# Phase B of a decoder layer on one core: another order of the slots around the step boundary

## The reference, cut to what matters

```
xn  = rmsnorm(layernorm(x)) ; mn = rmsnorm(memory)
q   = rope(xn @ q_w[h])            4 heads of 128
k   = rope(mn @ kv_w[0]) ; v = mn @ kv_w[1]      one head, shared
p   = softmax(mask(q @ k.T))       per head 512 x 512
enc = p @ v ;  out = x + sum_h enc[h] @ out_w[h]
```

## Time and profile before

| | |
|---|---|
| median of 3 runs | 3421.82 us (3419.85 to 3423.12) |
| profiled execution | 3417.78 us, its span 3416.0 us |
| mean granted PE clock | 0.976 |
| busy share of the span | PE 95%, PEld 79%, DVE 53%, ACT 40%, POOL 30% |
| phase B | about 1015 to 2045 us of the span, steps of 63.92 us |

### The profile page before, as it was taken

How to read it: one execution, slowest core, us unless ns; L and a number is a source line. 1 busy time by engine, 2 the same in 40 slices (tenths; PEclk the granted TensorE clock), 3 DMA queues, 4 the chain that set the end, 5 groups by cost and what they waited for, 6 DMA issues and landing times. The chain is left out here.

```text
span 3416.0 us, 41523 instructions
## 1 busy us (share of the span) xinstructions
PE 3231.5 (95%) x15856; PEld 2696.0 (79%) x15856; DVE 1814.0 (53%) x3793; ACT 1357.4 (40%) x2576; POOL 1024.2 (30%) x838
## 2 busy tenths in 40 slices
PE   7999999999958999999999987999999999999799
PEld 5888888888747878878878866888888888888687
DVE  5666666565547777777777754322322232221464
ACT  4444444444336666666666642221112111111233
POOL 1323232323226566565565540000000000000134
PEclk9999999999979999999999996999999999999899
DMA  2111112121131211211211103000000000000343
GB/s 102 38 52 60 59 53 69 43 73 39 50 107 52 88 64 51 88 64 51 88 64 51 62 25 112 24 24 14 13 13 25 13 13 13 25 1 0 127 161 135
DMA packets 102341, 188.28 MB, mean 55 GB/s; under 512 B 6912, under 2 KB 13056, under 8 KB 102144
## 3 DMA queue, kind: packets, MB, share of 16 engines
q1 hardware_dynamic: 102144, 185.63, 16.1%
HBM read 135.28 MB, written 50.33 MB: 54 GB/s over the span
## 5 line engine op out<-in xcount | busy, mean ns | idle before, releaser
L949 POOL TENSOR_SCALAR b_soft<-b_soft,b_one_in_sum 128x512 f32<-128x512 f32 x256 | 401.0, 1566 | 336.5 <-DVE b_one_in_sum L1116 336.5
L1490 ACT ACTIVATE c_gate<-c_g,c_bias 128x512 f32<-128x512 f32 x180 | 124.2, 690 | 754.1 <-PE c_g L131 754.1
L1513 DVE TENSOR_TENSOR c_gate<-c_gate 128x512 f32<-128x512 f32 x64 | 44.3, 692 | 570.9 <-ACT c_gate L1490 570.9
L287 POOL TENSOR_TENSOR kept_scale<-c_ln_ve,minus_half 128x4 f32<-128x4 f32 x16 | 16.1, 1009 | 961.9 <-DVE c_ln_ve L279 961.9
L1135 DVE TENSOR_TENSOR b_p_lo<-b_t,b_p_hi 128x512 fp32r<-128x512 f32 x256 | 175.1, 684 | 198.9 <-ACT b_p_hi L1001 197.1
L992 ACT ACTIVATE b_soft<-b_soft,b_minus_top 128x512 f32<-128x512 f32 x256 | 185.2, 724 | 232.0 <-DVE b_minus_top L1127 227.3
L480 ACT ACTIVATE a_elu<-a_p 128x512 f32<-128x512 f32 x128 | 76.5, 598 | 345.3 <-PE a_p L131 298.5
L1001 ACT ACTIVATE b_p_hi<-b_t 128x512 fp32r<-128x512 f32 x256 | 152.5, 596 | 102.4 <-PE b_t L1285 102.3
L1285 PE MATMUL b_t<-ident,b_soft 128*128 128x128 f32 x1024 | 157.8, 277 | 23.7 <-DVE b_p_lo L1135 23.7
L1660 POOL TENSOR_TENSOR d_x<-d_x,d_y 128x512 f32<-128x512 f32 x64 | 83.0, 1296 | 321.4 <-ACT d_y L1673 321.4
L1127 DVE CUSTOM_DVE_ANT_0 b_soft<-b_l,b_mask_row 128x512 f32<-128x512 f32 x256 | 175.2, 685 | 0.0
(11 more groups left out here) (303 smaller groups left out, 10153.5 us busy)
## 6 DMA issues: line engine op xcount, KB each, us to landing
a_x<-in_x SPq DMA_DIRECT2D x16, 1024.0 KB, 8.2
a_res<-in_x SPq DMA_DIRECT2D x16, 1024.0 KB, 6.4
x<-a_res SPq DMA_DIRECT2D x16, 1024.0 KB, 5.2
b_mem<-in_ctx SPq DMA_DIRECT2D x16, 1024.0 KB, 5.4
b_x<-x SPq DMA_DIRECT2D x16, 1024.0 KB, 5.5
b_res<-x SPq DMA_DIRECT2D x16, 1024.0 KB, 5.5
x<-b_res SPq DMA_DIRECT2D x16, 1024.0 KB, 4.3
c_x<-x SPq DMA_DIRECT2D x16, 1024.0 KB, 5.5
```

Source lines behind the costliest of these rows:

```text
L949: pool.tensor_scalar(soft[:, at, :], soft[:, at, :], one_in_sum[:, at:at + 1], None, ALU.mult).then_inc(p_norm.sem, p_norm.unit)
L1490: act.activation(gate[:, j % 2, i, :], gating.banks[(3 * j + i) % 6][:, :], ACT.Tanh if g == "c" else ACT.Sigmoid, bias=added[:, i, j:j + ...
```

## The change

Three moves, made alike on PE, ACT and DVE. `encode(old, 2)` goes from slot 15 to slot 14, and its `enc_high`/`enc_low` from slot 0 of the next step to slot 15. `encode(fin, 3)` goes from slot 1 to slot 0, `keys_values(0)` and `(1)` from slots 0 and 2 to slots 1 and 2, with the copies that follow them. The second pair of memory transposes goes from slot 14 to slot 15, and its `memory_high`/`memory_low` from slot 15 to slot 0 of the next step. `norm_apply` of tiles 2 and 3 moves from slot 2 to slot 1. No instruction is added or taken away.

```diff
@@ ACT
                         if fin:
                             if j == 0:
                                 p_high(fin.b, J - 1)
-                                enc_high(fin.b, 2)
-                            if j == 2:
+                            if j == 1:
                                 enc_high(fin.b, 3)
                         if old:
...
+                            if j == 15:
+                                enc_high(old.b, 2)
                         if new:
-                            if j == 1:
-                                values_high(0)
-                            if j == 3:
-                                values_high(1)
+                            if j == 0 and new.b >= 1:
+                                memory_high(s - 1, new.b, 2)
+                                memory_high(s - 1, new.b, 3)
+                            if j == 2 or j == 3:
+                                values_high(j - 2)
...
-                            if j == 14 or j == 15:
-                                memory_high(s, after, 2 * (j - 14))
-                                memory_high(s, after, 2 * (j - 14) + 1)
+                            if j == 14:
+                                memory_high(s, after, 0)
+                                memory_high(s, after, 1)
@@ PE
-                        if new and j == 0:
-                            keys_values(0)
-                        if fin and j == 1:
+                        if fin and j == 0:
                             encode(fin, 3)
-                        if new and j == 2:
-                            keys_values(1)
+                        if new and j in (1, 2):
+                            keys_values(j - 1)
...
-                        if following(new, B) and j in (13, 14):
-                            turn_memory(s, new.b + 1, 2 * (j - 13))
-                            turn_memory(s, new.b + 1, 2 * (j - 13) + 1)
-                        if old and j == 15:
+                        if following(new, B) and j in (13, 15):
+                            turn_memory(s, new.b + 1, j - 13)
+                            turn_memory(s, new.b + 1, j - 12)
+                        if old and j == 14:
                             encode(old, 2)
```

More of the change, by code:

```diff
@@ L1203, in step @@
                         if fin:
-                            if j == 0:
-                                enc_low(fin.b, 2)
-                            if j == 2:
+                            if j == 1:
                                 enc_low(fin.b, 3)
@@ L1212, in step @@
                                 enc_low(old.b, 1)
+                            if j == 15:
+                                enc_low(old.b, 2)
                         if new:
[L1214 to L1217, removed]
+                            if j == 0 and new.b >= 1:
+                                memory_low(s - 1, new.b, 2)
+                                memory_low(s - 1, new.b, 3)
+                            if j == 2 or j == 3:
+                                keys(j - 2)
                             if 4 <= j <= 7:
@@ L1243, in step @@
                                 self.norm_variance(dve, N, after)
-                            if j == 14 or j == 15:
-                                memory_low(s, after, 2 * (j - 14))
-                                memory_low(s, after, 2 * (j - 14) + 1)
+                            if j == 14:
+                                memory_low(s, after, 0)
+                                memory_low(s, after, 1)
                             if j == 15:
```

## The result

| | before | after |
|---|---|---|
| median | 3420.84 us (3419.81 to 3423.12, 4 runs) | 3441.61 us (3438.33 to 3446.04, 4 runs) |
| ratio | | 1.0061, 95% interval 1.0043 to 1.0078 |
| profiled execution, span | 3417.78, 3416.0 us | 3440.21, 3438.5 us |
| mean granted PE clock | 0.976 | 0.970 |

Slower by 0.6%, by the mechanism that was forecast and inside the range, with the price of the clock too small and the term for the ends of the wrong sign. The waits of PE in the steady part, as in the earlier trace rows: of the three old kinds none is left but b_t on p_lo, which has grown, and b_e on p_lo is new.

The account below looks back on a forecast made before the run. PE, busy 95% of the span, was taken to bound the kernel, losing 2.95 us per boundary to waits. Order +3.5, ends -1.6 and clock +9.6 gave +11.5 on 3417.78 us, 3433 us on the median; range 3418 to 3445.

Parts of the forecast that it names:

- the price of the clock: PE at a boundary where the clock falls to its lower level: 1.6 us per fall, range 0.9 to 1.9.
- the term for the ends: First and last boundaries of phase B, outside the steady ones: together -1.6 us.
- Slot 14 and slot 15: PE: encode(old, 2) hides slot 14's waits, but turn_p(15) stays at 1470.90 behind p_low(14), a stall of 1.71 us.
- Slots 0 to 2: PE: encode(fin, 3) stalls 1.48 us for p_low(15), until 1473.57; turn_x at 1485.48 against 1485.23, +0.25 us per boundary.
- the boundary into the step without a new item: End of phase B: gets the wait for p_low(15) with no keys to fill it, +0.7 us (0 to +1.5).
- the last step: End of phase B: shorter wait for enc_low(2) before encode(fin, 3), -1.3 us (0 to -2.0).
- the first boundary: Start of phase B, no fin: waits within keys_values(0) partly covered by the new order, -1 us (between 0 and -2.8).
- The clock: Steady boundaries: waits of 1.71 and 1.48 us close together make PE's clock fall at 6 of 14, +9.6 us.
- The sum: Whole kernel: +3.5 - 1.6 + 9.6 = +11.5 us on the profiled execution of 3417.78 us; chance 0.50.
- The clock that holds: Rival, steady boundaries: every boundary keeps the clock, +1.9 us, 3423.7 us, no measurable change; chance 0.30.
- The hidden waits: Rival, slots 15 and 0: p_low(14) and p_low(15) come as soon as transposes allow, -30 us, 3392 us; chance 0.08.
- The collision of DVE and POOL: Rival: POOL's L949 holds up norm_apply of the first tile, delaying p_low(15) by 0.45 us; +6.3, 3439 us; chance 0.12.

Follow-up runs that it names:

- the swap alone: Kernel before with only encode(old, 2) and the second memory turns exchanged between slots 14 and 15, head 2's copies in slot 15: 3417.89 us, ratio 0.9995.
- both waits filled: Changed kernel plus unused matmuls, 4 ahead of turn_p(15) and 5 ahead of encode(fin, 3): 3424.89 us, ratio 1.0015.
- the late copies: Changed kernel with the first two memory copies (high and low) moved from slot 14 to slot 0 of the next step: 3434.46 us, ratio 1.0038.
- and norm_apply: Changed kernel with the first two memory copies moved to slot 0, and norm_apply of tile 0 put behind p_low(15): 3409.05 us, ratio 0.9969.
- swap undone: Changed kernel with encode(old, 2) back in slot 15, second memory turns in slot 14, encode's head 2 copies in slot 0: 3435.56 us, ratio 1.0045.
- one of the two waits filled: Changed kernel plus 4 unused matmuls ahead of turn_p(15) only, the wait before encode(fin, 3) left idle: 3423.53 us, ratio 1.0013.
- late copies, filled: Changed kernel with the first two memory copies moved to slot 0, plus 5 unused matmuls ahead of encode(fin, 3): 3414.71 us, ratio 0.9985.
- p(15) first: On top of late memory copies and norm_apply behind p_low(15): p_high(15) before exp(new 1), p_low(15) before tile 1's reciprocal: 3397.09 us, ratio 0.9932.

## Why the prediction was right, and which terms were off

- *Slot 14 and slot 15.* Right to the hundredth: `turn_p(15)` at 1484.11 - 13.21 = 1470.90. That p_low(14)'s place behind memory_low sets it is shown: with the copies away the wait fell from 1.56 to 0.35, and the swap alone gathered the waits of slot 14 in slot 15 without shortening the step.
- *Slots 0 to 2.* Right with a small error: PE starts `encode(fin, 3)` at 1473.67, not 1473.57, since the hand-over from DVE took 0.84 here (p_lo at 1486.04, PE at 1486.88) and not 0.74, and it takes 2.83 for it, not 2.75. `turn_x` comes 0.41 later than before, not 0.25; the step is 64.29, not 64.2. Over 14 boundaries 5.2 in place of 3.5.
- *The ends.* Forecast -1.6, measured +2.2 up to step 1 and +0.3 behind step 14: the wrong sign, 4.1 off. Behind step 14 the terms came true: the boundary into the step without a new item +1.1 (forecast +0.7), the last step -1.2 (forecast -1.3), and 0.4 of the order. The miss is at the first boundary, forecast -1. The transposes of x at the start of phase B (1004.84 before, 1005.95 after) come 1.1 us later already, ahead of any moved instruction, with another low spell of the clock there. With both waits filled, where the first boundary is the same as in the changed kernel, the delay up to step 1 was 0.3 and not 2.2 (`turn_p(15)` at 1087.56 against 1087.24). So most of the 2.2 belongs to that execution and not to the order.
- *The clock.* That it would fall, and from what, was right: 7 boundaries of 14 fell, and none when the wait before `turn_p(15)` is filled or both are; filling the one before `encode(fin, 3)` alone was tried only with the late copies, where it ended all 12 falls. That it was 7 and the forecast 6 is luck: the 6 was chosen between bounds of 0 and 14, not worked out. **The term that was mis-sized is the price of a fall.** I took 1.6 us from a stretch of work of 4.0 us at the low level. Three falls cost that; the other four lasted twice as long, 6.8 us, and cost 2.9 each. The prediction had priced such a spell of 6.8 us at 3.4 at most and gave it little weight. The mean, 2.3, lies outside its 0.9 to 1.9. 7 falls cost 16.2, where 6 at 1.6 were to cost 9.6.
- *The sum.* On the profiled executions it was +22.4 us against a forecast of +11.5. The falls are 6.6 of the difference, the ends 4.1, the order 1.3 over 13 steps, and the later phases, which had no term, -1.0. The forecast was half the size of the measured change, and the range was wide enough to hold it.
- *The rivals.* The clock that holds is what the filled kernels show, 3423.5 and 3424.9 against the 3423.7 worked out for it (from +1.9, where the order alone costs 5). The hidden waits needed p_low(14) before the copies and p_high(15) before exp(new 1); with that order on ACT and DVE they come true, 3397 against 3392. The collision of DVE and POOL did not occur where I feared it: `norm_apply` of tile 0 took 0.54 at 1485.19, in the middle of POOL's L949 (1484.41 to 1486.20). Tile 1's, which no PE wait follows, did collide: at 1488.47, 1.05 us behind the start of the next L949, it took 0.80 and ended 0.29 behind L949's end, and so at all 14 boundaries. Of the exclusive lock for the whole instruction that the Trainium skill states (SBUF — State Buffer, on the shared port pair), the second case is as it says and the first is not. In which mode DVE ran these instructions no run shows.

## What to carry to other kernels

Moving the work of the engine that waits gained nothing here, because the wait was set by a place in another engine's queue. Look at what stands just ahead of the releasing instruction, without idle, and move that; then follow that engine's own waits in the new order, which is what the late copies missed. Where an order gathers PE's idle time in one place, look for the clock beside the sum of the idle time: here the step grew by 0.4 us, and the whole price was 1.6 us per boundary. Filling such a wait with matmuls whose results nobody uses is a cheap way to tell the two apart.

## What was not expected of the hardware

The table has PE's idles in us at one boundary, and at how many of the 14 boundaries the clock fell, in one profiled execution of each kernel:

| idle before `turn_p(15)`, before the next piece | falls |
|---|---|
| 1.56 and 1.41, 1.2 us of work between (the change) | 7 |
| 0.35 and 1.98 (copies late) | 12 |
| 0.31 and 1.41 (and norm_apply) | 1 |
| 1.56 and 0.62, 1.9 us of work between (swap only) | 0 |
| none (0.72 and 0.56 a slot before) and 1.93 (swap undone) | 1 |
| filled and 1.41 (one of the two waits filled) | 0 |
| 0.31 and filled (late copies, filled) | 0 |
| both filled | 0 |
| 0.31 and 0.81 (p(15) first) | 0 |

The idle per boundary alone does not order these rows: 2.97 us gave 7 falls and 2.33 gave 12. Why the copies-late kernel falls nearly every time is open.

POOL's scaling of a tile (L949) does not shut DVE out for its whole length. In the middle of it DVE's `norm_apply` took its usual 0.54 us, and POOL 1.79 in place of 1.57 (at 1484.41). Close behind its start DVE took 0.90 (at 1478.01 in the copies-late kernel), and late in it DVE was held until it ended (0.80 at 1488.47):

```profile
1484.41 1.79 POOL L949 TENSOR_SCALAR b_soft<-b_soft,b_one_in_sum 128x512 f32<-128x512 f32 x1
...
1487.42 1.56 POOL L949 TENSOR_SCALAR b_soft<-b_soft,b_one_in_sum 128x512 f32<-128x512 f32 x1
...
1488.47 0.80 DVE L293 TENSOR_SCALAR b_x<-b_x,b_ln_mv,b_n_scale 128x512 f32<-128x512 f32 x1
```
